# Second copies of four small buffers and a new order of steps in a two-layer cross-attention kernel

## The reference, cut to what matters

```
layer 0:  x = x + softmax(q k^T / 4) v  @ Wo.T + bo
layer 1:  probs_t  = softmax(q k_t^T / 4)                      (73 text tokens)
          text_out = probs_t v_t
          qsem     = l2norm(probs_t @ text)                    (needs the norm of a 512-wide vector per row and head)
          fused    = q k_ip^T / 4 + 0.5 * (qsem . l2norm(ip))
          ip_out   = (softmax(fused) * spatial_mask) v_ip
          x        = x + (text_out + ip_out) @ W_out + b_out
```

## Time and profile before

| | us |
|---|---|
| median of 3 runs | 2474.16 (2472.38 to 2474.91) |
| the profiled execution | 2473.34 |
| its span, first to last instruction | 2471.8 |

### The profile page before, as it was taken

The page is one execution under the profiler, slowest core; times in us unless marked ns, Lnnn a source line. Parts: engine busy times, 40 slices in busy tenths (PEclk is TensorE's granted clock), DMA queues, the critical chain, the costliest instruction groups (busy, mean ns, idle before and its releaser), DMA issues.

```text
span 2471.8 us, 90321 instructions
## 1 busy us (share of the span) xinstructions
PE 2273.8 (92%) x35896; PEld 1458.5 (59%) x35896; DVE 1699.8 (69%) x2860; ACT 1726.8 (70%) x2602; POOL 1593.7 (64%) x1056
## 2 busy tenths in 40 slices
PE   7899967999999999999999999999999999999984
PEld 5677744555555555556555555655556555556552
DVE  5534333777777777777777777777777777777763
ACT  3323325877777777778777778877787787787862
POOL 3212124777777777777777777777777777777762
PEclk9999978999999999999999999999999999999997
DMA  9677642444434444444444444444444444444431
GB/s 289 197 225 229 198 115 64 112 114 115 111 109 117 115 114 117 115 118 116 112 117 116 114 115 119 117 111 116 114 118 116 113 118 118 115 118 117 112 90 56
DMA packets 337787, 310.89 MB, mean 126 GB/s; under 512 B 180208, under 2 KB 280816, under 8 KB 337392
## 3 DMA queue, kind: packets, MB, share of 16 engines
q1 hardware_dynamic: 337392, 305.36, 44.0%
HBM read 164.66 MB, written 105.98 MB: 109 GB/s over the span
## 4 chain that ended last, share of the span: by engine, by line
PE 34%; DVE 18%; DMA 12%; ACT 8%; issue 6%; SPq 6%; POOL 1%; ACTq 0%; DVEq 0%; POOLq 0%
PE psum L933 8%; PE psum L1032 8%; DMA den<-ust 8%; PE psum L1016 6%; PE psum L995 5%; ACT ef L1121 5%; DVE mneg L1180 3%; DVE e L1202 2%; PE psum L936 2%; DVE sq L1221 2%; DVE ust L1269 2%; DVE outt L1280 2%; DMA pt<-p_dram 2%; PE psum L999 1%; PE psum L958 1%
## 5 line engine op out<-in xcount | busy, mean ns | idle before, releaser
L1348 POOL TENSOR_TENSOR e<-ef,eh 73x1024 f32<-73x1024 f32 x320 | 681.4, 2130 | 298.9 <-ACT eh L1136 261.9
L1121 ACT ACTIVATE ef<-psum 73x1024 f32<-73x1024 f32 (+1 forms) x640 | 628.5, 1012 | 104.8 <-PE psum L999 100.9
L1202 DVE TENSOR_TENSOR e<-psum,e 73x1024 f32<-73x1024 f32 x320 | 386.6, 1208 | 158.5 <-PE psum L1032 158.2
L1180 DVE TENSOR_REDUCE mneg<-psum 128x8 f16<-128x616 f32 (+3 forms) x512 | 448.2, 930 | 31.0 <-PE psum L958 30.2
L1032 PE MATMUL psum<-eh,gram 128*73 128x512 f16 x1280 | 337.6, 387 | 36.6 <-ACT ef L1121 12.7
L1016 PE MATMUL psum<-ef,values 128*32 128x256 f32 x5120 | 363.5, 389 | 8.0 <-DVE pip L1262 5.9
L995 PE MATMUL psum<-q_high,keys 32*73 32x256 f16 (+2 forms) x6144 | 325.5, 259 | 33.9 <-DVE mneg L1180 25.4
L1136 ACT ACTIVATE eh<-ef 73x1024 f16<-73x1024 f32 x320 | 337.0, 1053 | 16.4 <-ACT ef L1121 0.8
L995 PEld LDWEIGHTS psum<-q_high,keys 32*73 32x73 f16 (+1 forms) x6144 | 187.7, 111 | 143.6 <-issue 68.1
L1129 ACT ACTIVATE ust<-psum 128x512 f32<-128x512 f32 x384 | 228.2, 594 | 63.2 <-PE psum L1016 59.2
L1315 POOL TENSOR_TENSOR al<-ust,ah 128x768 f16<-128x768 f32 x128 | 210.7, 1646 | 86.6 <-ACT ah L1159 86.5
(11 more groups left out here) (180 smaller groups left out, 4659.7 us busy)
## 6 DMA issues: line engine op xcount, KB each, us to landing
rb<-r_dram SPq DMA_DIRECT2D x128, 384.0 KB, 3.8
keys<-k_dram SPq DMA_DIRECT2D x128, 231.0 KB, 3.7
values<-v_dram SPq DMA_DIRECT2D x128, 192.5 KB
ust<-ust SPq DMA_DIRECT2D x512, 48.0 KB, 2.1
v_dram<-vst SPq DMA_DIRECT2D x64, 320.0 KB
out<-outt SPq DMA_DIRECT2D x64, 320.0 KB, 2.3
k_dram<-kst SPq DMA_DIRECT2D x32, 616.0 KB, 3.9
x<-in_x SPq DMA_DIRECT2D x32, 384.0 KB, 3.7
```

What stands on the lines that cost most here:

```text
L1121: act.activation(ef[l][0:m, unit_heads(n), :].rearrange("t h s -> t (h s)"), src, ACT.Exp, scale=SM).then_inc(s_exp[l], 1)
L1180: dve.tensor_reduce(dst, o, AX_X, ALU.max, negate=True).then_inc(s_max[l], 1)
L1202: dve.tensor_tensor(rest, banks(l, f"u{k}", 2)[0:m, :, :], rest, ALU.mult).then_inc(s_wr, 1)
L1348: pool.tensor_tensor(e2[0:m, k, :, :], ef[1][0:m, unit_heads(k), :], eh[0:m, unit_heads(k), :], ALU.subtract).then_inc(s_e2, 1)
```

## The change

1. `gram`, `c4`, `vi` and `outt` are made twice, and picked by the batch's parity. The loads wait for the reader of two batches before, and for the previous load to have landed; the output step waits for the store of two batches before.
2. All five strings of `ORDER` and all eight lines of `USES` are new. The steps are the same, each once in a round, and the largest lag stays 4.

```diff
@@ ORDER, TensorE
-        1u2/3 1a1/3 0t1/1 1q/2 0t2/1 0a0/1 1s0/2 0a1/1 1s1/2 0a2/1 1i/2 1a2/3 1u3/3 1m/2 1u4/3 1t0/2 0q/0
-        1n0/3 1p/4 1n1/3 1n2/3 0s0/0 1n3/3 1n4/3 0s1/0 1t1/2 1a0/2 1u0/2 1t2/2 1u1/2 1o/4 0m/0 0o/1 0t0/0""",
+        1u2/3 1a1/3 0t1/1 1q/2 0t2/1 0a0/1 1a2/3 1s0/2 0a1/1 0a2/1 1s1/2 1u3/3 1n0/3 1n1/3 1n2/3 1i/2 1m/2
+        1p/4 1t0/2 1u4/3 0q/0 1n3/3 1n4/3 1a0/2 0s0/0 1t1/2 0s1/0 1u0/2 1o/4 1t2/2 0m/0 1u1/2 0o/1 0t0/0""",
...
@@ USES, the lines of banks 0, 2 and 4
+    "1a1/3 0a0/1 1s3/2 1p/4 1u4/3 0s1/0 0s2/0 1o/4 1u1/2",
...
+    "0t2/1 0t4/1 1s0/2 1s2/2 1p/4 1t2/2 1u0/2 0m/0 0t0/0",
...
+    "0t3/1 0t4/1 0a1/1 1u3/3 1t1/2 1a0/2 1t3/2 1t4/2 0t1/0",
...
@@ attention
-        gm = sb("gram", [P, 2, TXT[1]], F16)
-        c4 = sb("c4", [T, IP])
+        gm = sb("gram", [P, 2, 2, TXT[1]], F16)
+        c4 = sb("c4", [T, 2, IP])
...
-        vi = sb("vi", [IPR, D])
+        vi = sb("vi", [IPR, 2, D])
...
-        outt = sb("outt", [P, PW])
+        outt = sb("outt", [P, 2, PW])
...
             def load_gram(l, b, n):
-                b.reached(sp, f_u, UNITS, 0)
+                b.reached(sp, f_u, UNITS, -UNITS)
+                b.reached(sp, s_gm, 16, 0)
...
             def load_vip(l, b, n):
-                b.reached(sp, s_vb, 1, 0)
+                b.reached(sp, s_vb, 1, -1)
+                b.reached(sp, s_vi, 16, 0)
...
             def store(l, b, n):
                 b.reached(sp, s_xo[1], 1, 1)
+                b.reached(sp, s_store, 16, 0)
...
             def output(l, b, n):
-                    b.reached(dve, s_store, 16, 0)
+                    b.reached(dve, s_store, 16, -16)
```

More of the change, by code:

```diff
@@ L125 @@
     "pe": """
-        1u2/3 1a1/3 0t1/1 1q/2 0t2/1 0a0/1 1s0/2 0a1/1 1s1/2 0a2/1 1i/2 1a2/3 1u3/3 1m/2 1u4/3 1t0/2 0q/0
-        1n0/3 1p/4 1n1/3 1n2/3 0s0/0 1n3/3 1n4/3 0s1/0 1t1/2 1a0/2 1u0/2 1t2/2 1u1/2 1o/4 0m/0 0o/1 0t0/0""",
+        1u2/3 1a1/3 0t1/1 1q/2 0t2/1 0a0/1 1a2/3 1s0/2 0a1/1 0a2/1 1s1/2 1u3/3 1n0/3 1n1/3 1n2/3 1i/2 1m/2
+        1p/4 1t0/2 1u4/3 0q/0 1n3/3 1n4/3 1a0/2 0s0/0 1t1/2 0s1/0 1u0/2 1o/4 1t2/2 0m/0 1u1/2 0o/1 0t0/0""",
     "act": """
-        1a1/3 1f/4 0t2/1 0t3/1 1q/2 0t4/1 1h4/3 0a0/1 0a1/1 0a2/1 1i/2 1a2/3 1m/2 0r/0 1t0/2 1h0/2 0q/0
-        1t1/2 1h1/2 1n/3 1g/4 1t2/2 1t3/2 1a0/2 0g/1 1t4/2 1h2/2 0m/0 1r/2 1h3/2 0t0/0 0t1/0""",
+        1r/3 0t0/1 0t1/1 1f/4 0t2/1 0t3/1 1a1/3 1q/2 0t4/1 1a2/3 0a0/1 0a1/1 0a2/1 0r/0 1i/2 1m/2 1t0/2 1g/4
+        1t1/2 1h0/2 0q/0 1n/3 1a0/2 1h1/2 1t2/2 1h2/2 1t3/2 0g/1 1t4/2 1h3/2 0m/0 1h4/2""",
     "dve": """
-        1y11/4 0o/2 1y12/4 1y13/4 1y14/4 1w2/3 1y15/4 1y16/4 1y17/4 1y18/4 1y19/4 1ql/2 1s0/2 1s1/2 1s2/2
-        1s3/2 1w3/3 0d/1 1w4/3 1d/3 0ql/0 1p/4 0s0/0 0s1/0 0s2/0 0s3/0 1w0/2 1w1/2 1y0/3 1y1/3 1y2/3 1y3/3
-        1o/4 1y4/3 1y5/3 1y6/3 1y7/3 1y8/3 1y9/3 1y10/3""",
+        1y13/4 1y14/4 1y15/4 1w2/3 1y16/4 1y17/4 1y18/4 1y19/4 1ql/2 1s0/2 1s1/2 1s2/2 1s3/2 1w3/3 0d/1 1p/4
+        1w4/3 0ql/0 1d/3 0s0/0 0s1/0 0s2/0 0s3/0 1w0/2 1y0/3 1y1/3 1o/4 1y2/3 1y3/3 1y4/3 1y5/3 1y6/3 1y7/3
+        1y8/3 1y9/3 1y10/3 1w1/2 1y11/3 0o/1 1y12/3""",
     "pool": """
-        1xh/2 1xl/2 1b3/3 1b4/3 0xh/0 0xl/0 1vb/4 1kb/1 1at/4 1c/2 1b0/2 1b1/2 1al/4 0at/1 0al/1 1b2/2""",
+        1b3/3 1at/4 1vb/4 0xh/0 0xl/0 1b4/3 1kb/1 1al/4 1c/2 1b0/2 0at/1 0al/1 1b1/2 1b2/2 1xh/1 1xl/1""",
     "sp": """
-        1ss/3 1sl/3 1rl/4 1sh/4 0x/0 1vi/4 1ps/4 0ds/1 1v/2 1pl/4 1ds/3 0k/0 1g/2 0rw/1 0sh/1 0rl/1 1c/1
-        1ns/3 1rw/3 1nl/3 1k/1 1d/3 1st/4 0v/0""",
+        1sl/3 1rl/4 1sh/4 1ps/4 1c/2 1vi/4 0x/0 1pl/4 0ds/1 1ds/3 0v/0 1v/2 0k/0 0rw/1 0sh/1 0rl/1 1g/2
+        1ns/3 1nl/3 1d/3 1st/4 1k/1 1ss/2 1rw/3""",
 }
 USES = [
[8 rows of a table removed]
[8 rows of a table added]
 ]
@@ L825, in load_gram @@
                     sp.wait_ge(s_small, SMALL)
-                b.reached(sp, f_u, UNITS, 0)
+                b.reached(sp, f_u, UNITS, -UNITS)
+                b.reached(sp, s_gm, 16, 0)
                 src = g_dram[bass.DynSlice(b.index(), 1), :, :].rearrange("a t n -> (a t) n")
-                sp.dma_start(gm[0:T, :, :].rearrange("t h n -> t (h n)"), src).then_inc(s_gm, 16)
+                sp.dma_start(gm[0:T, b.parity(), :, :].rearrange("t h n -> t (h n)"), src).then_inc(s_gm, 16)
             def load_c4(l, b, n):
-                b.reached(sp, s_c4, 1, 0)
+                b.reached(sp, s_c4, 1, -1)
+                b.reached(sp, s_c4l, 16, 0)
                 src = c_dram[bass.DynSlice(b.index(), 1), :, :].rearrange("a t n -> (a t) n")
-                sp.dma_start(c4[:], src).then_inc(s_c4l, 16)
+                sp.dma_start(c4[:, b.parity(), :], src).then_inc(s_c4l, 16)
             def load_vip(l, b, n):
-                b.reached(sp, s_vb, 1, 0)
+                b.reached(sp, s_vb, 1, -1)
+                b.reached(sp, s_vi, 16, 0)
                 src = vip_dram[:, bass.DynSlice(b.index() * IP, IP), :].rearrange("c n (h d) -> c (n h) d", d=D)
-                sp.dma_start(vi[:], src).then_inc(s_vi, 16)
+                sp.dma_start(vi[:, b.parity(), :], src).then_inc(s_vi, 16)
             def move_denominators(l, b, n):
@@ L908, in store @@
                 b.reached(sp, s_xo[1], 1, 1)
+                b.reached(sp, s_store, 16, 0)
                 dst = out[bass.DynSlice(b.index(), 1), :, :].rearrange("a p n -> (a p) n")
-                sp.dma_start(dst, outt[:]).then_inc(s_store, 16)
+                sp.dma_start(dst, outt[:, b.parity(), :]).then_inc(s_store, 16)
             program("sp", {"x": load_x, "k": load_keys, "v": load_values, "g": load_gram, "c": load_c4,
@@ L1031, in gram_products @@
                     for half in (0, 1):
-                        mm = pe.matmul(banks(l, f"u{k}", 2)[0:n, r, :], gm[:, half, :], e, start=(half == 0),
+                        mm = pe.matmul(banks(l, f"u{k}", 2)[0:n, r, :], gm[:, b.parity(), half, :], e, start=(half == 0),
                                        stop=(half == 1))
@@ L1276, in output @@
                 else:
-                    b.reached(dve, s_store, 16, 0)
+                    b.reached(dve, s_store, 16, -16)
                 b.reached(dve, f_o[l], 1, 1)
-                dst, n = (xin[1][b.parity()][:].rearrange("p c s -> p (c s)"), CW * S) if l == 0 else (outt[:], PW)
+                dst, n = (xin[1][b.parity()][:].rearrange("p c s -> p (c s)"), CW * S) if l == 0 else (outt[:, b.parity(), :], PW)
                 dve.scalar_tensor_tensor(dst, row(l, "o", 2)[:, 0:n], 1 / WS, res[l][:, b.parity(), :], ALU.mult,
```

4 lines of the change are left out of this document (2 added, 2 removed), and 13 rows, old and new, of the table USES.

## The result

The changed kernel takes 2539.63 us (median of 4 runs, 2522.69 to 2552.07), the kernel before 2473.27 (2471.15 to 2474.91) on the same chip: 1.0269 times as long, with a 95% interval of [1.0246, 1.0293]. That is 66 us more, where 40 were forecast, inside the range of 2458 to 2542. The profiled execution of the changed kernel is its fastest run: 2522.69 us, with a span of 2520.7. The four runs go with the mean granted clock of their spans: 2522.69 at 0.979, 2539.34 at 0.976, 2539.92 at 0.974, 2552.07 at 0.969. The kernel before was profiled at 0.980.

What follows compares the result with a forecast made beforehand. TensorE's work plus its stalls bound the kernel: work falls 0.54 to 29.3 us, stalls rise from 1.8 to 3.0, so 0.63 more in each of 64 rounds, 40 us, gives 2514 us; range 2458 to 2542.

Steps and rivals of the forecast that it cites:

- TensorE's own work, 29.3 us: TensorE's work per round falls by 0.54 us, mainly because pieces of the sums' shape fall from eight to five.
- The copies, 0 us: Second copies of four buffers gain nothing, as rounds did not wait for their transfers; bounds -5 and +2 us.
- 1, `1u3`: `1u3` shares bank 4 with `0a1`, whose sums ACT reads late: 0.11 us of stall.
- 2, `1t0`: `1t0` waits for the turned maxima, with the image scores ahead on ACT: 0.15 us of stall.
- 3, `1u4`, `0q`: `1u4` waits for DVE's reading of `p`, `0q` for the exponentials of `1t0`: 0.05 and 0.33 us.
- 4, `1t1`: `0s0` waits 0.03 us for low queries; `1t1` waits 0.70 for bank 4, just filled by `1a0`.
- 5, `1u0`: `0s1` waits 0.04 us for maxima; `1u0` waits 0.92 for banks 2 and 3, holding `1t1`'s products.
- 6, `1u1`: `1u1` shares banks 0 and 1 with `1o` and waits for DVE's output: 0.45 us of stall.
- 7, `1u2`: `1u2`, at the round's end, waits for layer 0's output: 0.20 us of stall.
- the second rival, the late probabilities: Image probabilities (`pt`) land late for `p`, up to 1 us a round: 32 us more, 2530 to 2570; chance 0.11.
- Drains bound it: Saved shape changes count and stalls stay at 1.8 us: 35 us less, 2440, partly 2435 to 2467; chance 0.17.
- Both cancel: Stalls of 2.3 to 2.4 us a round offset the saved work: 2469 to 2479 us; chance 0.09.

Runs made afterwards that it cites:

- e4: The changed kernel with ACT reading the sums `1a0` twice: 2590.21 us, 1.0484 times the kernel before.
- e8: The changed kernel with `0a2` moved behind the second scores of layer 1, six pieces of sums instead of five: 2548.95 us, 1.0313 times the kernel before.
- e2: The kernel before with only the second copies of the four small buffers added, orders as before: 2470.78 us, 1.0000 times the kernel before.
- e1: The changed kernel run once more, nothing altered: 2535.65 us, 1.0273 times the kernel before.
- e12: The changed kernel with `0r` moved behind `0g` on ACT and six unused products filling the stall ahead of `1u0`: 2523.24 us, 1.0222 times the kernel before.
- e11: The changed kernel with `0r` moved on ACT from ahead of `1i` and `1m` to behind `0g`: 2543.66 us, 1.0307 times the kernel before.
- e6: The changed kernel with six unused products filling the stall ahead of `1u0`: 2529.50 us, 1.0234 times the kernel before.
- e9: The changed kernel with the load of `pt` issued ahead of the load of `x`: 2639.25 us, 1.0671 times the kernel before.
- e5: The kernel before with ACT reading the sums `1a0` twice: 2479.21 us, 1.0035 times the kernel before.

## Why the prediction was right, and where its size was off

**What bounds the kernel.** Right. A round is TensorE's work and stalls, and nothing else: e4 lengthens one link of it by 0.48 and the round grows by 0.48.

**TensorE's own work, 29.3 us.** Right. The quiet round less its stalls is 32.33 - 2.99 = 29.34; this is a remainder and not measured apart. A piece of 24 takes 1.43 to the next start (1433.40 to 1434.83), as the text said, and e8 prices a piece at 0.16. Of what it named as proof against itself, nothing came.

**The copies, 0 us.** Right: e2.

**The new stalls, 3.0 us.** Right, term by term, each as the step's distance to the next start less what it takes where nothing is waited for:

| term | forecast | measured, how |
|---|---|---|
| 1, `1u3` | 0.11 | 0.12: 1436.50 to 1436.92, less 0.30 |
| 2, `1t0` | 0.15 | 0.13: 1439.88 to 1440.65, less 0.64 |
| 3, `1u4`, `0q` | 0.38 | 0.38: 1.08 less 1.00, 1.19 less 0.89 |
| 4, `1t1` | 0.73 | 0.78: 1447.22 to 1448.25, less 0.25 |
| 5, `1u0` | 0.96 | 0.99: 1449.22 to 1450.52, less 0.31 |
| 6, `1u1` | 0.45 | 0.38: 0.51 less 0.13 |
| 7, `1u2` | 0.20 | 0.21: 1.21 less 1.00 |
| sum | 3.0 | 2.99 |

The releasers are those named: `ACT ust`, `ACT ef`, `DVE outt`. That the sums agree to 0.01 is luck in part: terms 4 and 5 came 0.08 too small together, term 6 0.07 too large. The forecast's round of 32.3 us is the measured 32.33. Its "0.63 more" is 0.71, which is 5 us over 64 rounds. The new stalls are right to 0.01, so the 0.08 lies in the work saved (0.54) or in today's stalls (1.8, of which the text adds up 1.64 and puts the rest at "two of some 0.09"). The terms could not carry the second decimal.

**The step that was mis-sized is the last one: "64 x 0.63 = 40 us ... I leave them as they are".** It takes each round for a quiet one, and what disturbs rounds for the same as before. The median is 66 us above before. The profiled run nearest to it is e1's, 61.3 us longer than before by its span; in brackets the first profile, 48.9 us longer:
- Quiet rounds: 64 x 0.71 = 45, in both (forecast 40).
- Falls of the clock behind the two large stalls: 13 (4), put at nothing. A round with one is 1.68 us longer (34.01 against 32.33). Of the 12.4 us between the two profiled runs 9.1 lie in rounds with a fall. With the stall filled, and no fall left behind `1u0`, 20 us went (e12 against e11, same chip and hour) or 6 to 10 (e6 against e1). The prediction read the clock at 1.00 in the earlier trace rows and took it for a property of the kernel; it is one of the order.
- The two ends, beyond the three quiet rounds in them: 4 (2), put at 0, plus or minus 6.
- The other disturbed rounds, late transfers among them: 1 less than before (2 less).
- `x` late for `0r`, and so `1t0` late: nothing that the times show. TensorE waited 3.9 and 2.5 us for `ACT mt` in the profiles of the changed kernel and e1, but the rounds without a fall are 12.0 and 13.1 us above quiet there, and 14.8 and 16.0 in e11 and e12, where those waits are gone. It is a risk all the same that the prediction did not see, and e9 shows its price. The walk gave `mt` "the image scores ahead", but not `0r`, which the new order also put there. It had judged the new place of the loads by POOL, as "nothing is later by it", and not by ACT.

No execution at the median of 2539.63 itself was profiled. That it lies in the stated range, 2.4 us below its upper end, is luck in part: that end came from the second rival, the late probabilities, and the clock, which brought the time there, was in no term.

**The rivals.** *Drains bound it* is out: the drains are real and the work fell, but the stalls are 2.99 and the turning point was 2.34. *Late probabilities* is there in small: 5.7 us of waits in the profile, 7.7 to 17.1 in e1, e6, e11 and e12, 2.6 before, and not the 32 that it was priced at. It would not have been told from the clock by the time alone. *Both cancel* is out. I gave the right case 0.63; its own range, 2498 to 2530, held the profiled run but not the median.

**What stays open.** Why the clock falls behind `1u0` in one round in nine and not in the others, where the two stalls are nearly always the same to 0.01 us. Whether it is the standing still or the smaller amount of work in that stretch that counts: the filling changes both. Why the clock stood low for longer at the end of e11 than of e1. And where e5's 9 us went.

## What to carry to other kernels

When an order is judged by TensorE's work, also list the last reader of each bank and the distance from writer to writer. Here two writers put too close behind a reader cost 1.8 us a round, where the stalls at these two steps had been 0.8, and joining shapes saved some 0.5. Stalls that stand close together can cost twice, the second time through the clock; here a pair of 0.7 and 0.9 us came before the falls, where about the same sum spread over the round had not. And a step that waits for a load is safer behind the steps that TensorE waits for than ahead of them: moving it gained nothing here while the load was in time, but a load that came 2 us later cost 100 us.

## What the runs showed of the hardware that I had not expected

- The granted clock of a kernel whose TensorE is busy for 89% of the span falls in full flow: 7 times in 61 rounds in e1 (89%), 21 in e4 (88%), none before (92%) or in e12 (91%). Each of e1's falls starts behind a pair of stalls (0.71 and 0.92 us, 1.3 us of work between), holds 3.4 us, once 6.8, at 1.2 GHz, and costs 1.7 us, the long one 2.7.
- Six products whose result nobody reads, put in the place of a stall, leave the quiet round as it is and make the kernel faster: with `0r` moved by 0.8% (1.0307 [1.0283, 1.0330] to 1.0222 [1.0199, 1.0244], same chip and hour), without by 0.4% (1.0273 [1.0256, 1.0289] to 1.0234 [1.0215, 1.0252], the intervals just apart).
- The load of `pt` (4.3 us from issue to landing) is as slow without the load of `x` ahead of it. In the traces it lands in 4 steps of its semaphore and `x` in 16; whether this is why was not tested.
